# A decoder layer with a state space mixer: how the mixer's state entries, its Toeplitz blocks and its token statistics are made

## What is computed

```python
x = x + mixer(layernorm(x))            # mixer: see below
x = x + cross_attention(ctx, ctx, layernorm(x))
x = x + ffn(layernorm(x))              # 256 -> 2 x 1024, silu gate, two 1024 x 1024 gelu layers, -> 256

def mixer(x):
    xn = (x - mu) / sqrt(var + eps) * ln_gamma + ln_beta
    dt = exp(log_dt); dA = exp(-exp(log_A) * dt[:, None]); dB = B * dt[:, None]
    h = dA * h + dB * u[..., None]     # one step for each token, 64 states for each of 256 features
    y = einsum('dn,bdn->bd', C, h) + D * u
    return x + y_all @ W_out + b_out
```

## Time and profile before

| | |
|---|---|
| median of 3 runs | 933.9 us |
| the profiled execution | 934.08 us, span 932.3 us |
| TensorE busy | 869.6 us (93%), mean granted clock 0.981 |
| VectorE, ScalarE, GpSimd busy | 514.6, 493.6, 183.2 us |
| first record of the core | 51.43 us |
| last evacuation of the core starts | 102.39 us |

### The profile page before, as it was taken

The page is one execution under the profiler, slowest core; times in us unless marked ns, Lnnn a source line. Parts: engine busy times, 40 slices in busy tenths (PEclk is TensorE's granted clock), DMA queues, the critical chain, the costliest instruction groups (busy, mean ns, idle before and its releaser), DMA issues.

```text
span 932.3 us, 15096 instructions
## 1 busy us (share of the span) xinstructions
PE 869.6 (93%) x5570; PEld 697.0 (75%) x5570; DVE 514.6 (55%) x927; ACT 493.6 (53%) x761; POOL 183.2 (20%) x201
## 2 busy tenths in 40 slices
PE   1168999899999999999999999999999999999997
PEld 0068867677777778777877887778778777777886
DVE  7987485465446464555555555554555456553411
ACT  2927533476356735764475536653575366635432
POOL 1567800500041002200230014000500050003000
PEclk9679999999999999999999999999999999999999
DMA  9961797500110002000200010001100110001000
GB/s 340 243 162 55 261 387 306 226 1 1 52 45 0 0 22 73 0 0 15 81 0 0 0 73 22 0 0 51 45 0 0 51 45 0 0 23 45 1 1 25
DMA packets 15497, 61.79 MB, mean 66 GB/s; under 512 B 2835, under 2 KB 4502, under 8 KB 14646
## 3 DMA queue, kind: packets, MB, share of 16 engines
q1 hardware_dynamic: 15430, 61.31, 19.0%
q0 software_dynamic: 32, 0.00, 0.0%
HBM read 49.63 MB, written 23.20 MB: 78 GB/s over the span
## 4 chain that ended last, share of the span: by engine, by line
PE 89%; DVE 5%; issue 4%; ACT 1%; POOL 0%; DMA 0%; SPq 0%; DVEq 0%; POOLq 0%
PE pair L1342 51%; PE pair L1329 11%; PE pair L1354 6%; PE pair L1269 4%; PE pair L1280 3%; PE pair L1296 3%; PE pair L470 2%; PE pair L477 2%; PE pair L1289 1%; PE pair L1319 1%; PE pair L1236 1%; PE pair L484 1%; PE pair L539 1%; DVE GG L337 1%; DVE stn L343 1%
## 5 line engine op out<-in xcount | busy, mean ns | idle before, releaser
L950 ACT ACTIVATE vbuf<-pair,scl 128x512 f32<-128x512 f32 x128 | 87.8, 686 | 231.0 <-PE pair L1342 222.1
L1342 PE MATMUL pair<-h2hi,h_turned 128*128 128x512 f32 x512 | 202.6, 396 | 0.0
L1342 PE MATMUL pair<-h2lo,h_turned 128*128 128x512 f32 x512 | 199.6, 390 | 0.0
L1342 PE MATMUL pair<-h1hi,h_turned 128*128 128x512 f32 x384 | 153.1, 399 | 0.0
L1342 PE MATMUL pair<-h1lo,h_turned 128*128 128x512 f32 x384 | 150.0, 391 | 0.0
L1118 DVE TENSOR_TENSOR h1lo<-vbuf,h1hi 128x512 fp32r<-128x512 f32 x80 | 57.7, 722 | 120.1 <-ACT h1hi L951 119.3
L1342 PEld LDWEIGHTS pair<-h2hi,h_turned 128*128 128x128 f32 x512 | 96.2, 188 | 25.2 <-issue 5.9
L1342 PEld LDWEIGHTS pair<-h2lo,h_turned 128*128 128x128 f32 x512 | 96.2, 188 | 19.3
L1118 DVE TENSOR_TENSOR h2lo<-vbuf,h2hi 128x512 fp32r<-128x512 f32 x64 | 44.2, 691 | 107.2 <-ACT h2hi L951 107.1
L1329 PE MATMUL pair<-zThi,w_turned 128*128 128x512 f32 x224 | 92.0, 411 | 2.9 <-DVE vbuf L1142 2.9
L1142 DVE SCALAR_TENSOR_TENSOR vbuf<-pair,scl,sg 128x512 f32<-128x512 f32 x64 | 47.9, 750 | 80.5 <-ACT sg L939 60.8
(11 more groups left out here) (145 smaller groups left out, 1593.3 us busy)
## 6 DMA issues: line engine op xcount, KB each, us to landing
h_turned<-d_h SPq DMA_DIRECT2D x2, 4096.0 KB, 15.1
xres<-in_x SPq DMA_DIRECT2D x8, 512.0 KB, 7.5
tok<-in_xs SPq DMA_DIRECT2D x8, 512.0 KB, 12.2
EE<-alpha_rows SPq DMA_DIRECT2D x16, 256.0 KB, 10.7
ring<-kernel_rows SPq DMA_DIRECT2D x16, 256.0 KB, 4.3
xr<-x_rows SPq DMA_DIRECT2D x8, 512.0 KB, 3.5
out<-xr SPq DMA_DIRECT2D x16, 256.0 KB, 2.1
x_rows<-xres SPq DMA_DIRECT2D x7, 512.0 KB, 12.4
```

The source lines that it names most:

```text
L950: e.activation(vb[:, s % 2, :], h_ps[s % 4], ACT.Gelu, scale=sc)
L1342: ins = e.matmul(bank, w[:, k, m * P:(m + 1) * P], src[part][:, k, :], start=(k == 0 and part == 0), stop=(k == HC - 1 and part == 1))
```

## The change

The diff, cut to its core:

```diff
+STAGE = {0: 3, 4: 0, 1: 2, 5: 1, 2: 3, 3: 2, 6: 0, 7: 3}
+EXP_AT = {g: n + 1 for n, g in enumerate(STAGE)}
 LAG = 2
-ACT_SHARE = 20
+ACT_SHARE = 18
+ACT_STATS = (8, 16)
+ROWS_AT = 3
+PAD = 2 * L
...
+    ttw = [nc.alloc_sbuf_tensor_at(f"tt{k}", [P, GRP * PAD], F32, offset=t[n]) for k, n in enumerate(("w1_at", "w2_at", "w3_at"))]
+    TT_AT = [(ring, 0), (ring, GRP * PAD)] + [(w, 0) for w in ttw]
+    TT = [w[:, at:at + GRP * PAD] for w, at in TT_AT]
+    ksb = nc.alloc_sbuf_tensor_at("ksb", [P, 2, BLK], F32, offset=t["w3_at"])
...
-        e.wait_ge(coef, 2)
-        for u in range(2):
-            e.dma_start(alS[P * (1 - u):P * (2 - u), :], al2[:, u, :]).then_inc(al_st, 16)
...
+        e.wait_ge(const, 10)
+        for u in range(4):
+            e.dma_start(kr[0, L * u * PAD:L * (u + 1) * PAD].rearrange("(c m) -> c m", m=PAD)[:, L:PAD], rev[0:L, L:P]).then_inc(kr_zero, 16)
...
+        for h in range(2):
+            e.wait_ge(k_ev, h + 1)
+            for v in range(4):
+                c = (P * (1 - h) + 32 * v) * PAD
+                e.dma_start(kr[0, c:c + 32 * PAD].rearrange("(q c m) -> q c m", q=4, c=8)[:, :, 0:L],
+                            ksb[v:P:32, h, :].rearrange("q (c m) -> q c m", c=8)).then_inc(kr_st, 16)
+        e.wait_ge(kr_st, 128)
+        e.wait_ge(kr_pad, 16)
+        e.wait_ge(kr_zero, 64)
+        for g in range(5):
+            tt_load(e, g)
...
+        for g in range(5, NGRP):
+            e.wait_ge(w_ps, 2 * (g - 5) + 2)
             tt_load(e, g)
...
+        e.wait_ge(w_ps, NOCT)
...
+        e.wait_ge(d_in, 32)
+        e.wait_ge(w_row, 2)
+        e.wait_ge(g_row, 7)
+        for row in (0, N):
+            v = GG[row:row + 1, :, L - 1]
+            e.tensor_tensor(v, v, edit[row:row + 1, 0, :], ALU.add).then_inc(d_add, 1)
+        e.wait_ge(d_add, 2)
+        power(0)
+        e.wait_ge(k_ps, 1)
+        e.wait_ge(powd, 1)
+        for row in (0, N):
+            e.tensor_copy(GG[row:row + 1, :, L - 1], edit[row:row + 1, 1, :]).then_inc(g_back, 1)
+        e.wait_ge(g_back, 2)
+        power(1)
...
+        e.wait_ge(g_row, 1)
+        for row in (0, N):
+            e.activation(edit[row:row + 1, 1, :], GG[row:row + 1, :, L - 1], ACT.Copy).then_inc(w_row, 1)
+
+        def tile_stats(first, until):
+            here, n = slice(first, until), until - ACT_STATS[0]
+            e.wait_ge(xr_in[first // 4], 16)
+            if n > 4:
+                e.wait_ge(t_var, n - 4)
+            for j in range(first, until):
+                e.activation(junk[j % 4], xres[:, j, :], ACT.Copy, accum_out=tsum[:, 0, j:j + 1]).then_inc(t_sum, 1)
+            e.wait_ge(t_sum, n)
+            e.activation(tsum[:, 1, here], tsum[:, 0, here], ACT.Copy, scale=-1.0 / (16 * DM)).then_inc(t_mean, 1)
+            e.activation(mvn[:, here, 0], tsum[:, 0, here], ACT.Copy, scale=1.0 / DM).then_inc(t_mean, 1)
+            e.wait_ge(t_mean, n // 2)
+            for j in range(first, until):
+                e.activation(junk[j % 4], xres[:, j, :], ACT.Square, bias=tsum[:, 1, j:j + 1], scale=1.0 / 16, accum_out=mvn[:, j, 1:2]).then_inc(t_var, 1)
...
+                if c == ROWS_AT:
+                    row_evac()
...
-            e.wait_ge(E_in[g], 32)
-            v = EE[:, GRP * g:GRP * g + GRP, :].rearrange("p d n -> p (d n)")
-            e.activation(v, v, ACT.Exp, scale=esc[:, :]).then_inc(e_rdy, 1)
+            e.wait_ge(e_ps, g % 4 + 1)
+            e.activation(EE[:, GRP * g:GRP * g + GRP, :].rearrange("p d n -> p (d n)"), pair[STAGE[g]][:, :], ACT.Exp, scale=esc[:, :]).then_inc(e_rdy, 1)
...
-        for v in range(4):
-            row_evac(v)
-        e.wait_ge(const, 9)
+        e.wait_ge(const, 10)
+        tile_stats(8, 12)
+        for g in (0, 4):
+            entry_exp(g)
+        tile_stats(12, 16)
+        for g in (1, 5, 2):
+            entry_exp(g)
         norm_apply(0)
-        entry_exp(0)
         norm_apply(1)
-        for g in range(1, 3):
+        for g in (3, 6, 7):
...
             entry_exp(g)
...
+            if b == 0:
+                e.wait_ge(t_var, ACT_STATS[1] - ACT_STATS[0])
...
-        stats(4, 8)
+        stats(4, ACT_STATS[0])
+        last_two(0)
         double(5)
-        e.wait_ge(d_in, 32)
-        e.wait_ge(d_add, 2)
-        e.wait_ge(g_row, 7)
-        for row in (0, N):
-            v = GG[row:row + 1, :, L - 1]
-            e.tensor_tensor(v, v, edit[row:row + 1, 0, :], ALU.add).then_inc(d_add, 1)
-        stats(8, 16)
         variances(0)
-        stats(16, 26)
+        stats(SB, SB + 8)
         spreads(0)
-        stats(26, 32)
+        stats(SB + 8, TILES)
+        last_two(1)
         variances(1)
         e.tensor_scalar(svn[:, :], mvn[:, :, 1], EPS, None, ALU.add).then_inc(nat_v, 1)
-        for k in range(2):
-            e.memset(hps[k], 0.0).then_inc(h_zero, 1)
         norms(0)
         spreads(1)
-        e.wait_ge(k_ps, 4)
-        for row in (0, N):
-            e.tensor_copy(GG[row:row + 1, :, L - 1], edit[row:row + 1, 1, :]).then_inc(g_row, 1)
-        e.memset(dec[:, :, 0], 0.0).then_inc(dec0, 1)
         e.wait_ge(bc_in, 64)
         gamma(0)
-        norms(1)
         beta(0)
         gamma(1)
         beta(1)
+        norms(1)
         gamma(2)
         beta(2)
...
         e.wait_ge(g_row, 7)
-        e.wait_ge(d_add, 4)
+        def spread_entries(n):
+            for i in range(GRP):
+                for g, h, u in ((n, 0, 0), (n + 4, 1, 1), (n, 1, 0), (n + 4, 0, 1)):
+                    rows, c = slice(N * u, N * u + N), GRP * g + i
+                    ins = e.matmul(pair[STAGE[g]][L * h:L * h + L, N * i:N * i + N], ident[rows, c:c + 1].to_broadcast([N, L]), al2[rows, 1 - h, :], start=True, stop=True)
+            ins.then_inc(e_ps, 1)
+        spread_entries(0)
+        e.wait_ge(pk_done, 7)
+        e.wait_ge(w_row, 2)
+        spread_entries(1)
+        e.wait_ge(e_rdy, EXP_AT[4])
+        spread_entries(2)
+        e.wait_ge(d_add, 2)
+        e.wait_ge(e_rdy, EXP_AT[5])
         for v in range(4):
-            if v >= 2:
-                e.wait_ge(k_ev, 2 * v - 2)
             for q in range(4):
                 for h in range(2):
                     c = (v * 32 + q * 8) * L
-                    ins = e.matmul(kps[v % 2][h][32 * q:32 * q + 32, :], ones[N * h:N * h + N, 0:32], GGf[N * h:N * h + N, c:c + 8 * L], start=True, stop=True)
-            ins.then_inc(k_ps, 1)
+                    ins = e.matmul(kps[h][32 * q:32 * q + 32, :], pick[N * h:N * h + N, 3 - v:35 - v], GGf[N * h:N * h + N, c:c + 8 * L], start=(v == 0), stop=(v == 3))
+        ins.then_inc(k_ps, 1)
+        e.wait_ge(e_rdy, EXP_AT[2])
+        spread_entries(3)
+        e.wait_ge(k_ev, 2)
+        e.wait_ge(dec0, 1)
+        e.wait_ge(z_b, 2)
+        for k in range(5):
+            e.matmul(hps[k % 2].rearrange("p (a d) -> p a d", a=4), ident[:, :], dec[:, :, 0].unsqueeze(1).to_broadcast([P, 4, P]), start=True, stop=True)
...
-                e.wait_ge(t_mask, o + 2)
+                e.wait_ge(xr_T_in[o // 2 % 5], 16 + 32 * (o // 10 + 1))
             if o + 1 < NOCT and o % 2 == 1:
-                e.wait_ge(e_rdy, o // 2 + 2)
+                e.wait_ge(e_rdy, EXP_AT[o // 2 + 1])
             if o + 1 < NOCT and o % 4 == 3:
                 e.wait_ge(z_b, (4, 6, 8)[o // 4])
             if o >= 1:
                 e.wait_ge(h_scan, o)
+            if o == 0:
+                e.wait_ge(e_rdy, EXP_AT[3])
             if o == 1:
-                e.wait_ge(g_row, 9)
+                e.wait_ge(g_back, 2)
+            if o == 2:
+                e.wait_ge(e_rdy, EXP_AT[6])
```

More of the change, by code:

```diff
@@ L79, in mixer_parts @@
     rev = sb("rev", [P, P], "c")
-    ones = sb("ones", [P, 32], "c")
+    pick = sb("pick", [P, 35], "c")
     stn = sb("stn", [P, TILES, 6], "d")
@@ L140, in tt_load @@
         for h in range(2):
[L141 to L147, removed]
+            e.dma_start(TT[g % 5][L * h:L * h + L, :],
+                        bass.AP(t["kr_h"], (8 * h + g) * (GRP * PAD), [[1, L], [1, GRP * PAD]])).then_inc(xr_T_in[g % 5], 16)
     def sync_mixer(e):
@@ L204, in x1_store @@
         e.dma_start(x1d[i], xres[:, 4 * i:4 * i + 4, :].rearrange("p j d -> p (j d)")).then_inc(x1_st, 16)
[L206 to L210, removed]
-            e.affine_select(out=v, in_=v, compare_op=ALU.is_ge, fill=0.0, base=L - 1,
-                            pattern=[[0, GRP], [-1, L]], channel_multiplier=-1).then_inc(t_mask, 1)
     def bias(e, tile):
@@ L220, in gpsimd_prep @@
         e.memset(rev[:, :], 0.0).then_inc(const, 1)
-        e.memset(ones[:, :], 1.0).then_inc(const, 1)
+        e.memset(pick[:, :], 0.0).then_inc(const, 1)
         e.memset(mhalf[:, :], -0.5).then_inc(const, 1)
@@ L230, in gpsimd_prep, with power @@
             blk = rev[64 * h:64 * h + 64, 64 * h:64 * h + 64]
-            e.wait_ge(const, 7 + h)
+            e.wait_ge(const, 8 + h)
             e.affine_select(out=blk, in_=blk, compare_op=ALU.not_equal, fill=1.0, base=-63,
```

(27 more changed lines are left out.)

83 lines of the change are left out of this document (36 added, 47 removed).

## The result

The changed kernel takes 947.8 us (median of 4 runs, 947.2 to 949.09), the kernel before 934.25. The ratio is 1.0149, 95% interval 1.0128 to 1.017: slower by 13.5 us. The forecast had the direction and both places of the loss, and less than half of its size. The profiled execution took 949.09 us with a span of 947.4, so 15.1 us more span than before.

The account below looks back on a forecast made before the run. The prediction took TensorE's chain as the bound, with VectorE bounding the preparation ahead of the core. Core start 58.0 + 42.9 + 7.5 stalls = 108.4 against 102.4, so 934.1 + 6.0 = 940.0 us; range 929 to 948.

Parts of the forecast that it names:

- the wait and what hangs on it: Preparation: TensorE's first spread waits for the last doubling, delaying ScalarE's statistics, so VectorE idles 11 us.
- the row products and the spreads: TensorE's preparation: row products take 6.6 to 6.8 us, a spread 3.4 us at 26 ns a record.
- the zero products: Five products ahead of the core, from 50.7, ending between 57.2 and 58.5; core start taken as 58.0.
- the stalls in the core: Instruction blocks come late while the data queue is full, costing the core 7.5 us.
- The undisturbed core: Core without stalls or clock loss: first state 0.9, 15 x 2.6, plus 3.0, giving 42.9 us.
- the sum: Core end 58.0 + 42.9 + 7.5 = 108.4 against 102.4, 6.0 us later; time 940.0 us.
- My own bounds: Core stalls: 4 to 5 blocks, each 1.3 to 2.9 us late, given as 5 to 13 us.
- The start of the core at half clock: The core's first 5.7 us ran at clock 0.50 before, about 2.8 us lost, regained with a full clock.
- The second: Rival: instruction blocks come in time in the core, no change, 934 us, range 931.5 to 936.5; chance 0.2.
- The third: Rival: block transfers done before an earlier, undisturbed core, 930.9 us, down to 926; chance 0.2.
- The fourth: Rival: dear statistics passes, or five blocks in the core each 2.9 us late, about 949 us; chance 0.15.
- dear statistics: Rival's part on ScalarE: each statistics pass costs 1.04 us, 4 us more ahead of VectorE's wait; shared chance 0.15.

Follow-up runs that it names:

- e1: Changed kernel without TensorE's wait for the last doubling ahead of spread 0: 941.39 us, ratio 1.0068 to the kernel before.
- e3: Changed kernel without the Toeplitz block loads of groups 2 to 7, same products on wrong blocks: 932.03 us, ratio 0.997 to the kernel before.
- e4: Kernel before, with the 4 MB weight copy within HBM issued after 11 octets instead of 16: 941.38 us, ratio 1.0072.
- e5: Changed kernel with each block load cut into two transfers of 4 KB per partition, same bytes: 946.17 us, ratio 1.0112 to the kernel before.
- e11: Changed kernel without the block loads of groups 2 to 7 and with two zero products instead of five: 930.13 us, ratio 0.9947.
- e2: Changed kernel with the padding alone undone: 4 MB of blocks, masked on GpSimd again: 941.7 us, ratio 1.0067 to the kernel before.
- e9: Changed kernel without the wait ahead of spread 0, padding undone, GpSimd's masks held until the third beta: 928.98 us, ratio 0.9934.
- e12: Changed kernel without the wait ahead of spread 0, padded rows read without their zeros, 4 MB in 256-byte pieces: 930.3 us, ratio 0.9947.
- e8: Changed kernel with ScalarE's second four tiles of statistics ahead of its first two exponentials, wait left in: 948.63 us, ratio 1.0145.

## Why the prediction was right or wrong

**Right: the wait and what hangs on it.** The last doubling ended at 18.98 (19.1 forecast), spread 0 began at 19.04 (19.2), exponential 0 at 22.80 (22.7), the eight tiles were ready at 28.9 (29.9), VectorE idled 9.99 us (11). e1 shows the cause. ScalarE's passes cost 0.31 us and 0.09 for the accumulator's record (start to start 0.40 for the sums, 0.49 for the squares), below the 0.56 that I took.

**Mis-sized: the row products and the spreads.** I took 6.6 to 6.8 us for 64 records from the kernel before; they took 3.66. I took 26 ns for a spread's record; the first spread ran at 29, the second, at a clock of 0.50, at 27, the last, 128 records in 2.09 us at 1.00, at 16. The clock of 1.00 that I read beside the row products before was no measurement: that trace has no record of the clock until 26.4 us, and a window without one shows 1.00. The shorter row products and the shorter passes made the third beta end at 53.2, not 56.6.

**Wrong in its parts, right in its end: the zero products.** They ran from 47.18 to 56.08, 0.86 us a record. I had 0.45 from a projection with full rows, and 0.9 only at half clock. Their weight loads start 0.86 us apart both at 49, where the clock is 0.50, and at 53, where it is 1.00: the rate did not follow the clock. What else holds them (their moving operand is read with a step of 64 bytes) was not tested. The core started at 56.02 against 58.0.

**The step that failed: the stalls in the core.** The mechanism, instruction blocks that come late beside data transfers, stands: e3 takes the transfers away and the stalls go, e4 adds some and stalls come, the instruction packets end just ahead of TensorE's return in every stall, and halving the rows (e5) changes little. Its size was wrong: 42.9 + 7.5 = 50.4 us were forecast, 61.05 came. The 10.7 us between them are three terms. The stalls were 12.7 us and not 7.5, which is 5.2. The undisturbed core takes 44.7 (e3) and not 42.9, which is 1.8. And 3.7 us stand beside the stalls, most of it under the half clock, for which the sum had nothing.

On the stalls: the transfers ran at 197 to 246 GB/s and kept the queue full until 74, not 70. TensorE stood up to 4.25 us at an instruction block, where I had 1.3 to 2.9. My own bounds, 4 to 5 blocks of 1.3 to 2.9 us, reach from 5 to 14.5 us, not 13, and I chose 7.5 because bursts behind 70 us have gaps. They had gaps (a DMA share of 0.57 and 0.62 in the windows from 74 to 82), and three of the five stalls, 6.7 us, ended behind 74 all the same. On the clock: behind the stalls of 1.80, 4.25, 2.76 and 2.91 us it stood at 0.50 for 3.4 us each. Before, the same pair can be read in the earlier trace rows: the stall of 2.79 us with the clock at 0.50 behind it. I had given it 1.4 us in the account of the kernel before and named "a halved clock behind the longest" for the changed one, but put it at nothing in the sum.

In terms of the sum: 56.0 + 44.7 + 12.7 + 3.7 = 117.1, the measured end. The start that came 2.0 us earlier than forecast hid a part of the miss. The start of the core at half clock, which I priced at 2.8 us, cost 0.3 where it could be compared (e3 and e11). The rule of the Trainium skill that I set against it ("Runtime: NRT & Kernel Launch", "Instruction fetch mechanics": crossing a block is mostly hidden) holds here only with an empty queue, as in e3 and e11; with a full one the trace has 11.5 to 14.3 us of stalls.

**The rivals.** The second needed blocks that come in time while the queue is full; they did not. The third needed a queue that is done before the core; it was not. The fourth had the size (949) by "five blocks each 2.9 us late", 0.15 as a chance: the five stalls of the core had 2.5 us on average, and the slower core beside them did the rest. The other half of that rival, dear statistics, was wrong. The median lies 0.2 us inside the upper end of the range, 948.

**What the forecast did not see at all** is what undoing the padding costs: it counted the masks only on the betas (2.04 against 1.21 us), while 14 chunks beside ten masks go from 3.68 to 12.56 us. Against e2's order, to have no masks beside these chunks was worth 8.9 us; its price was paid in a queue that no engine's busy time shows. e9 has the same 3.67 us for the chunks without the padding, by holding the masks until the third beta.

## What to carry to other kernels

A stretch of unrolled small products needs its instructions through the same DMA engines as the data: add the transfers that fall into it, look for idle places marked "issue" beside bursts and for a packet of the instruction queue that ends just ahead of TensorE's return, and count each with the half clock behind it (about 0.7 us for a block of 256 records here). Few engines busy is no sign of safety: in e4 one engine's last packet was enough. Finish bulk loads before such a stretch, or carry fewer bytes (e12: the same layout read without its zeros was worth 11.1 us). Before an order is tuned, look for a wait that its instruction does not need: one line was worth 6.4 us here, and reordering around it nothing (e8).

## What the runs showed of the hardware

- An instruction block came in one packet of 16 KB, for 256 records of TensorE's matmuls and weight loads. With the queue empty it began 0.4 to 1.3 us after the previous block had begun to run (e3); TensorE used up 256 records in 3.4 to 4.1 us there. With the queue full it began up to 5.9 us after (after).
- The same spread of 128 records took 3.40 us at 27 us, with a clock of 0.51 in the window from 27 to 30, and 2.09 us at 35, with 1.00. The first spread took about 3.8 us at 19 us, and the row products 6.59 us before and 3.66 after. In both slow cases TensorE had done nothing for 13 us or more, and neither trace has a record of the clock yet (the first are at 26.4 us before and 23.1 after). In e9 they took 5.31 us, from 22.11 us on, and the clock changed within them:

```profile
22.11:25.50 3.39, 3.39 (x33) 0.99 (x41) 3.13 (x17) 1.86 (x4) 1.30 (x1) 0.50 1.04 391
25.60:27.40 1.80, 1.80 (x44) 0.40 (x28) 1.80 (x11) 0.16 (x1) 0.00 (x0) 1.00 0.93 244
```

  An estimate: with 57 ns a record at full clock (3.66 / 64) and twice that at half, e9 comes to 5.4 us, and the row products before, if at half clock until 26.4 us, to 6.6. So the half clock fits both, though no record shows it there. The row products before also waited for their evacuations.
- `tensor_scalar` on VectorE, with one input in SBUF, went from 0.26 to 0.90 us for each 128x128 chunk beside GpSimd's `affine_select`; the scans, which read PSUM, stayed at 1.34 to 1.36 us, beside the masks of e9 too.
- Blocks, 8 MB in all, moved in rows of 8 KB at 211 to 224 GB/s (windows of 4 us from 46 to 74 us but for one of 258), and in rows of 4 KB at 214 to 223 but for one of 253; pieces of 256 bytes reached 167 to 172.
